# First layer's bias as a 127th row of the units' weights, and one activation per stage

## The chip, the core and the metric

One core of a Trainium2 chip runs the kernel. The metric is the time of one execution on the device in microseconds (us), the median of the runs. All work is inside one launch. The engines are TensorE (PE; its weight loads are the separate row PEld), VectorE (DVE), ScalarE (ACT), GpSimd (POOL), which here issues the gathers, and SyncE (SP), which issues all other transfers. Each engine runs its own list of instructions in order and waits on semaphores that others raise.

## What is computed

The tower of a recommendation model over a batch of 2048. 26 rows of 128 floats are looked up in 26 tables by id; together with the dense features that makes 27 vectors a sample. All pairs of them are multiplied (the interactions), and a three-layer network follows.

```python
e = jnp.stack([tbl_0[ids[:, 0]], ..., tbl_25[ids[:, 25]]], axis=1)
combined = jnp.concatenate([dense_features[:, None, :], e], axis=1)       # 2048 x 27 x 128
interactions = jnp.einsum('bnd,bmd->bnm', combined, combined)
z = jnp.concatenate([dense_features, interactions[:, _TRIU_I, _TRIU_J]], axis=1)
h = jnp.concatenate([z, r_dense_features], axis=1)
h = jnp.maximum(h @ W_top1 + b_top1, 0.0)      # 607 -> 512
h = jnp.maximum(h @ W_top2 + b_top2, 0.0)      # 512 -> 256
y = h @ W_top3                                 # 256 -> 1
```

## The kernel before

The batch is cut into 8 groups of 256 samples, each of two tiles of 128. Of the 26 tables 17 are gathered by GpSimd, one indirect DMA for each table and tile (272 in all, L372), into `rows`, which has a place for each of a group's two tiles. TensorE turns the gathered rows over (`transposes`, L626, five banks a tile), and a place may be filled again once the transposes that read it two tiles earlier are done (the wait in `gather`, L369). The other nine tables, of 1000 rows, are looked up by matmul: VectorE builds a one-hot matrix from the ids (L523), and TensorE multiplies it with the table, split into a high and a low part (`look_up`, L659). ScalarE and VectorE copy the results from PSUM into `embed_t`. TensorE then forms the interactions (`gram`, L689), and ScalarE (L439) and VectorE (L512) copy them out as "units", 14 x 27 = 378 numbers a sample. They go to DRAM and back (`bounce`, L302 and L306), so that they lie as 3 chunks of 126 rows: `packed_raw` in `scratch`.

The network of a group runs during the next group, in seven stages M0 to M6. M0 to M3 are the first layer's four blocks of 128 outputs, M4 and M5 the second layer's two, M6 the last. All float32 products are made of three float32r products (high x high, low x high, high x low; L695 to L697), so each operand is split into a high part (a cast on ScalarE, or an activation with that type) and a low part (VectorE subtracts the high part from the whole, `lower`, L534). A stage M0 to M3 ends with two activations on ScalarE: L401 writes relu(x + b1) in full to `hidden1_raw`, which lies in `scratch`, and L402 the same as `hidden1_hi`; VectorE then makes `hidden1_lo` out of the two. Each stage writes one of two banks of `mlp_ps`, by turns; the bank with the odd stages is also used by the odd ones of the nine look-ups (H1, H3, H5, H7), so a look-up there waits until the stage before it has been copied (L656).

What an engine does in which order is set by one list for all engines, two lines a group, one for each tile:

```python
STEPS = [
    "G0 S0 Q0 H0 M0 Q1 Q2 H1 G1 W0 Q3 H2 W1 M1 Q4 M2 W2 H3 W3".split(),
    "G0 M3 Q0 H4 W4 M4 D0 E0 Q1 Q2 H5 W5 G1 Q3 H6 M5 Q4 H7 H8 M6".split(),
]
```

G is a round of interactions, Q a bank of transposes, H a look-up and the making of a later one-hot, M a stage, S and D the splits of units and dense features, E the dense columns' place in `embed_t`, W the split of a piece of the network's weights, in group 0 only, when there is no stage yet. The last group has a list of its own and two more banks for its stages.

The weights come in once. After the last hot table has been split, SP issues the three loads of `w1_units` (L333), one for each chunk, 126 rows of 512 floats each; two land in `scratch`, one in a buffer of `units`. ScalarE's split of the first one (W0, `weights_upper`, L476) waits for all three: `act.wait_ge(pieces_loaded, 16 * CHUNKS)`. When VectorE has split all three, SP loads `w2` to `scratch`, and when that is split, `w_dense` and `w_again` (L336 to L340).

Of the kernel before, what the change touches and what calls it, by code (L numbers as in the profile page):

```python
# [71 lines left out]
UNIT_P = UNITS * N // CHUNKS  # L72
H1, H2 = 512, 256
# [33 lines left out]
def dlrm_tower(nc, dense_t, ids, hot_ids, row_numbers, tables, w1_dense, w1_again, w1_units, b1, w2, b2, w3, identity, late_rows, bounce, y):  # L107
    ctx = ExitStack()
    with ctx:
# [14 lines left out]
        w1u_hi = sb("w1u_hi", [UNIT_P, CHUNKS, H1], F32R)  # L124
        w1u_lo = sb("w1u_lo", [UNIT_P, CHUNKS, H1], F32R)
# [3 lines left out]
        b1_sb = sb("b1_sb", [P, H1_CHUNKS], F32)  # L129
# [12 lines left out]
        packed_hi = sb("packed_hi", [UNIT_P, BLOCK, CHUNKS, GROUP_BLOCKS], F32R)  # L142
        packed_lo = sb("packed_lo", [UNIT_P, BLOCK, CHUNKS, GROUP_BLOCKS], F32R)
# [14 lines left out]
        hidden1_raw = scratch[:, 0:2, :]  # L158
# [53 lines left out]
        units_lo = sem("units_lo")  # L212
        hidden1_split = sem("hidden1_split")
# [5 lines left out]
        pieces = [(landing[c][0:UNIT_P], w1u_hi[:, c, :], w1u_lo[:, c, :]) for c in range(CHUNKS)]  # L219
# [58 lines left out]
        def _(sp):  # L278
# [45 lines left out]
            sp.dma_start(b1_sb[:, :], b1).then_inc(weights_loaded, 16)  # L324
# [61 lines left out]
        def _(act):  # L386
# [5 lines left out]
            def mlp_copy(g, buf, m):  # L392
# [37 lines left out]
            def units_upper(g, landing=packed_raw):  # L430

                act.wait_ge(units_packed, 16 * (g + 1))
                nc.scalar.copy(packed_hi[:, :, :, :], landing).then_inc(units_hi, 1)
# [40 lines left out]
            def weights_upper(n):  # L474
                if n < CHUNKS:
                    act.wait_ge(pieces_loaded, 16 * CHUNKS)  # L476
                elif n == CHUNKS:
                    act.wait_ge(weights_loaded, 16 * 4)
# [21 lines left out]
            for c in range(CHUNKS):  # L500
                nc.scalar.copy(packed_hi[:, :, c, :], last_packed_raw[:, :, c, :]).then_inc(last_units_hi, 1)
# [4 lines left out]
        def _(dve):  # L506
# [38 lines left out]
            def units_lower(g, landing=packed_raw):  # L545

                dve.wait_ge(units_hi, g + 1)
                lower(landing, packed_hi[:, :, :, :], packed_lo[:, :, :, :]).then_inc(units_lo, 1)

            def hidden1_lower(g, m):  # L550
# [3 lines left out]
                lower(hidden1_raw[:, m % 2, :], hidden1_hi[:, m, :], hidden1_lo[:, m, :]).then_inc(hidden1_split, 1)  # L554

            def group(g, buf, steps, mlp_before=True):
                for t2 in range(TILES):
                    for step, n in [(x[0], int(x[1:])) for x in steps[t2]]:
# [20 lines left out]
                        elif step == "W" and not mlp_before:  # L579

                            dve.wait_ge(weights_loaded, 16 * 6)
# [16 lines left out]

            dve.wait_ge(late_loaded, 16)
# [5 lines left out]
            for c in range(CHUNKS):  # L605
                dve.wait_ge(last_units_hi, c + 1)
                lower(last_packed_raw[:, :, c, :], packed_hi[:, :, c, :], packed_lo[:, :, c, :]).then_inc(last_units_lo, 1)
# [4 lines left out]
        def _(pe):  # L612

            odd_bank = {"tables": 0, "stages": 0}
# [24 lines left out]
            def look_up(g, n):  # L639
# [59 lines left out]
            def mlp(g, buf, m):  # L699
# [36 lines left out]
            def last_mlp():  # L736
# [20 lines left out]
                for part in (range(H1_CHUNKS - 1), range(H1_CHUNKS - 1, H1_CHUNKS)):  # L757
                    for m in range(H1_CHUNKS, H1_CHUNKS + H2_CHUNKS):
                        if part[0] == 0:

                            pe.wait_ge(mlp_copied, MLP_USES * g + m - H1_CHUNKS + 2)
# [40 lines left out]
            pe.wait_ge(weights_loaded, 16 * 6)  # L802
# [63 lines left out]
```

## Time and profile before

| | |
|---|---|
| runs | 392.56, 392.69 and 388.4 us, median 392.56 |
| the profiled execution | span 391.2 us |
| TensorE, its weight loads | 334.4 us busy (85%), 299.1 (76%) |
| VectorE | 260.1 us (66%) |
| ScalarE | 184.1 us (47%) |
| GpSimd | 272.6 us (70%) |
| moved by DMA | 33.28 MB, mean 85 GB/s |

The profile shows one execution. The share of an engine is its busy time over the whole span; how full it is in a part of the program has to be read from a table by stretches. GpSimd's idle time lies in pieces of 0.3 us between gathers. In the chain that ended last, followed back from the end, GpSimd has 40% of the span, TensorE 28%, VectorE 6%, and 16% is "issue", time in which the engine on the chain waited for nothing that the profile shows.

### The profile page before, as it was taken

The page shows a single profiled execution, that of the slowest core. Times are in us where ns is not written, and L with a number is a line of the kernel's source. Part 1 is how long each engine was busy: PE and PEld are TensorE (multiplying, and loading weights), DVE is VectorE, ACT ScalarE, POOL GpSimd, SP SyncE. Part 2 cuts the span into 40 slices and gives each one's busy share as a digit, 9 for nine tenths or more (in the row PEclk, how much of TensorE's full clock was granted, in tenths as well). Part 3 has the DMA queues.
Part 4 walks back from the last instruction along what each step waited for, and adds up shares of the span by engine and source line. Part 5 has one row for each costly group of instructions (what it writes and reads, how often), then busy time and mean ns, then how long its engine had stood idle before and what let it go on. Part 6 is the DMA issues. An engine that isn't in the chain of part 4 may idle for free.

```text
span 391.2 us, 13472 instructions
## 1 busy us (share of the span) xinstructions
PE 334.4 (85%) x6164; PEld 299.1 (76%) x6164; DVE 260.1 (66%) x203; ACT 184.1 (47%) x281; POOL 272.6 (70%) x277
## 2 busy tenths in 40 slices
PE   1866895949999999999998998999989998984847
PEld 1755885839999899889987987878878887873746
DVE  5799697765868876768677765867577665542211
ACT  3454542515464545454554546454535356444314
POOL 6778777777777777777777777777777777773000
PEclk9999998887999999999999999999999999998879
DMA  7971424341225221332133122422133121411020
GB/s 196 263 187 49 129 57 131 97 138 51 57 55 149 57 56 50 116 90 57 49 110 102 51 56 70 139 53 56 50 119 93 50 55 50 141 52 34 3 88 0
DMA packets 19047, 33.28 MB, mean 85 GB/s; under 512 B 5989, under 2 KB 11857, under 8 KB 18992
## 3 DMA queue, kind: packets, MB, share of 16 engines
q0 software_dynamic: 8768, 17.88, 17.5%
q1 hardware_dynamic: 10224, 14.55, 12.6%
q8 instruction: 49, 0.80, 0.9%
q14 instruction: 6, 0.05, 0.0%
HBM read 28.77 MB, written 3.68 MB: 83 GB/s over the span
## 4 chain that ended last, share of the span: by engine, by line
POOL 40%; PE 28%; issue 16%; DMA 6%; DVE 6%; ACT 2%; POOLq 0%; SPq 0%; DVEq 0%
POOL rows L372 40%; PE hot_ps L659 6%; PE mlp_ps L659 5%; PE gram_ps L689 4%; DVE one_hot L523 3%; PE transpose_ps L626 3%; PE mlp_ps L695 3%; DMA rows<-table,ids_sb 3%; PE mlp_ps L696 2%; PE mlp_ps L697 2%; PE hot_ids_ps L635 1%; DVE units L512 1%; DMA scratch<-w 1%; DMA scratch<-w_again 1%; DMA rows<-bounce 1%
## 5 line engine op out<-in xcount | busy, mean ns | idle before, releaser
L372 POOL DMA_INDIRECT rows<-table,ids_sb x272 | 271.7, 999 | 83.4 <-issue 82.3
L523 DVE TENSOR_TENSOR one_hot<-hot_ids_ps,row_numbers_sb 125x2048 fp32r<-125x2048 f32 x72 | 165.0, 2296 | 68.7 <-PE hot_ids_ps L635 62.4
L659 PE MATMUL hot_ps<-one_hot,table_hi 125*128 125x256 f32 x320 | 84.1, 299 | 6.5 <-DVE table_lo L534 4.2
L659 PE MATMUL hot_ps<-one_hot,table_lo 125*128 125x256 f32 x320 | 80.9, 289 | 0.0
L659 PE MATMUL mlp_ps<-one_hot,table_hi 125*128 125x256 f32 x256 | 66.1, 295 | 4.2 <-issue 3.7
L659 PEld LDWEIGHTS hot_ps<-one_hot,table_hi 125*128 125x128 f32 x320 | 63.2, 197 | 8.3 <-issue 8.3
L659 PE MATMUL mlp_ps<-one_hot,table_lo 125*128 125x256 f32 x256 | 63.9, 286 | 0.0
L659 PEld LDWEIGHTS hot_ps<-one_hot,table_lo 125*128 125x128 f32 x320 | 63.4, 198 | 0.0
L626 PE MATMUL transpose_ps<-identity_sb,rows 128*128 128x128 f32 x272 | 46.1, 291 | 18.7 <-DMA rows<-table,ids_sb 13.7
L689 PE MATMUL gram_ps<-embed_t 128*27 128x27 f32 x4096 | 53.5, 195 | 8.8 <-issue 2.3
L390 ACT COPY embed_t<-transpose_ps 128x512 f32<-128x512 f32 (+1 forms) x48 | 54.7, 1139 | 13.2 <-PE transpose_ps L626 12.6
L689 PEld LDWEIGHTS gram_ps<-embed_t 128*27 128x27 f32 x4096 | 44.8, 106 | 19.8 <-issue 13.2
L659 PEld LDWEIGHTS mlp_ps<-one_hot,table_hi 125*128 125x128 f32 x256 | 49.7, 194 | 5.8 <-issue 5.8
L626 PEld LDWEIGHTS transpose_ps<-identity_sb,rows 128*128 128x128 f32 x272 | 30.6, 144 | 28.3 <-DMA rows<-table,ids_sb 22.7
L445 ACT COPY embed_t<-hot_ps 128x256 f32<-128x256 f32 x40 | 27.2, 681 | 51.0 <-PE hot_ps L659 51.0
L512 DVE COPY_PREDICATED units<-late_sb,gram_ps 128x208 f32<-128x208 int32 x32 | 35.3, 1104 | 23.6 <-ACT units L439 23.3
L659 PEld LDWEIGHTS mlp_ps<-one_hot,table_lo 125*128 125x128 f32 x256 | 49.9, 195 | 0.0
L439 ACT COPY units<-gram_ps 128x224 f32<-128x224 f32 x32 | 18.0, 564 | 46.8 <-PE gram_ps L689 46.8
L445 ACT COPY embed_t<-mlp_ps 128x256 f32<-128x256 f32 x32 | 21.9, 683 | 27.6 <-PE mlp_ps L659 27.6
L695 PE MATMUL mlp_ps<-packed_hi,w1u_hi 126*128 126x256 f32 x90 | 26.9, 299 | 7.7 <-DVE packed_lo L534 7.7
L530 DVE COPY embed_t<-transpose_ps 128x384 f32<-128x384 f32 x32 | 32.8, 1025 | 0.0
L696 PE MATMUL mlp_ps<-packed_lo,w1u_hi 126*128 126x256 f32 x90 | 26.1, 291 | 0.0
(70 smaller groups left out, 386.0 us busy)
## 6 DMA issues: line engine op xcount, KB each, us to landing
rows<-table,ids_sb POOLq DMA_INDIRECT x272
embed_t<-table SPq DMA_DIRECT2D x8, 448.0 KB
bounce<-units SPq DMA_DIRECT2D x8, 448.0 KB, 2.7
scratch<-bounce SPq DMA_DIRECT2D x7, 378.0 KB
dense_sb<-dense_t SPq DMA_DIRECT2D x8, 128.0 KB
scratch<-w SPq DMA_DIRECT2D x1, 512.0 KB, 4.0
scratch<-w_units SPq DMA_DIRECT2D x2, 252.0 KB
scratch<-table SPq DMA_DIRECT2D x1, 448.0 KB
```

The source lines that it names most:

```text
L372: nc.gpsimd.indirect_dma_start(rows[:, t2, f - 1, :], None, tables[table], bass.IndirectOffsetOnAxis(ids_sb[:, tile, table:table + 1], 0)) ...
L390: nc.scalar.copy(embed_target(g, t2, u), embed_source(t2, u)).then_inc(even_copied, 1)
L439: nc.scalar.copy(unit_slot(buf, r, 0, UNITS), gram_slot(r, HALF, N)).then_inc(late_copied, 1)
L445: nc.scalar.copy(out, hot_bank(k).rearrange("p (t b) -> p t b", t=TILES)).then_inc(hot_copied, 1)
L512: nc.vector.copy_predicated(unit_slot(buf, r, 1, UNITS), rows_taken, gram_slot(r, 0, HALF)).then_inc(early_copied, 1)
L523: nc.vector.tensor_tensor(one_hot[:, k % RING], ids.to_broadcast([HOT_P, HOT_STEPS, GROUP]), row_numbers_sb[:, :, None].to_broadcast([HOT_ ...
L530: nc.vector.tensor_copy(embed_target(g, t2, u), embed_source(t2, u)).then_inc(odd_copied, 1)
L626: last = nc.tensor.transpose(transpose_ps[:, (t2 * TILE_BANKS + u) % 2, i, :], rows[:, t2, f - 1, :], identity_sb[:, :])
L659: last = nc.tensor.matmul(hot_bank(n), table[:, n, step, :], one_hot[:, k % RING, step, :], start=(step == 0 and table is table_hi), stop= ...
L689: last = nc.tensor.matmul(gram_ps[32 * s:32 * s + N, r % 2, q * N:(q + 1) * N], embed_t[:, slot, b, :], embed_t[:, slot, b, :], start=True ...
L695: nc.tensor.matmul(out, w[0], x[0], start=start, stop=False)
L696: nc.tensor.matmul(out, w[0], x[1], start=False, stop=False)
```

## The change

- The bias of the first layer becomes a 127th row of the units' weights. `w1_units` gets three more rows, one for each chunk: the first holds the bias, the others zeros. The three loads and the splits take 127 rows instead of 126.
- `packed_hi` and `packed_lo` get a 127th row as well, set once by VectorE ahead of group 0: ones in the high part, zeros in the low part. The memsets begin at row 96; the copies of the units write rows 0 to 125 over it later. The matmuls of the units contract over 127 rows instead of 126.
- ScalarE runs one activation in M0 to M3 instead of two (no bias, no `hidden1_raw`), and no longer waits for VectorE there.
- VectorE makes `hidden1_lo` as max(x, 0) minus the high part, with x read from the stage's bank in PSUM.
- So TensorE waits for VectorE's low part where it waited for ScalarE's activation: ahead of stages M2 to M5, and ahead of a look-up in the odd bank.
- The load of the bias, `b1_sb`, is dropped; counts of `weights_loaded` go down by one.

```diff
+BIAS_P = UNIT_P + 1
+ONES_AT = 96
...
-        w1u_hi = sb("w1u_hi", [UNIT_P, CHUNKS, H1], F32R)
+        w1u_hi = sb("w1u_hi", [BIAS_P, CHUNKS, H1], F32R)
...
-        packed_hi = sb("packed_hi", [UNIT_P, BLOCK, CHUNKS, GROUP_BLOCKS], F32R)
+        packed_hi = sb("packed_hi", [BIAS_P, BLOCK, CHUNKS, GROUP_BLOCKS], F32R)
...
-        pieces = [(landing[c][0:UNIT_P], w1u_hi[:, c, :], w1u_lo[:, c, :]) for c in range(CHUNKS)]
+        pieces = [(landing[c][0:BIAS_P], w1u_hi[:, c, :], w1u_lo[:, c, :]) for c in range(CHUNKS)]
...
-            sp.dma_start(b1_sb[:, :], b1).then_inc(weights_loaded, 16)
...
-                    if m >= 2:
-
-                        act.wait_ge(hidden1_split, H1_CHUNKS * g + m - 1)
-                    nc.scalar.activation(hidden1_raw[:, m % 2, :], src, ACT.Relu, bias=b1_sb[:, m:m + 1])
-                    nc.scalar.activation(hidden1_hi[:, m, :], src, ACT.Relu, bias=b1_sb[:, m:m + 1]).then_inc(mlp_copied, 1)
+                    nc.scalar.activation(hidden1_hi[:, m, :], src, ACT.Relu).then_inc(mlp_copied, 1)
...
-                lower(hidden1_raw[:, m % 2, :], hidden1_hi[:, m, :], hidden1_lo[:, m, :]).then_inc(hidden1_split, 1)
+                nc.vector.scalar_tensor_tensor(hidden1_lo[:, m, :], mlp_bank(g, m), 0.0, hidden1_hi[:, m, :].bitcast(F32),
+                                               ALU.max, ALU.subtract).then_inc(hidden1_split, 1)
...
+            nc.vector.memset(packed_hi[ONES_AT:BIAS_P, :, :, :].bitcast(F32), 1.0).then_inc(ones_set, 1)
+            nc.vector.memset(packed_lo[ONES_AT:BIAS_P, :, :, :].bitcast(F32), 0.0).then_inc(ones_set, 1)
...
                     pe.wait_ge(mlp_copied, odd_bank["stages"])
+                    pe.wait_ge(hidden1_split, odd_bank["splits"])
...
+                    odd_bank["splits"] = H1_CHUNKS * g + min(m + 1, H1_CHUNKS)
+                if 2 <= m < H1_CHUNKS + 2:
+
+                    pe.wait_ge(hidden1_split, H1_CHUNKS * g + m - 1)
...
-    w1_units = np.zeros((UNITS * N, H1), w1.dtype)
-    w1_units[where >= 0] = w1[where[where >= 0]]
+    w1_units = np.zeros((UNITS * N + CHUNKS, H1), w1.dtype)
+    w1_units[:UNITS * N][where >= 0] = w1[where[where >= 0]]
+    w1_units[UNITS * N] = a["b_top1"]
```

SP's list around the loads of the weights, before (`w_units` is the DRAM tensor of the units' weights, `w` is w2):

```order
L287 DMA dense_sb<-dense_t 128x256
L333 DMA scratch<-w_units 126x512 [waits lo_split]
L333 DMA scratch<-w_units 126x512
L333 DMA units<-w_units 126x512
L336 DMA scratch<-w 128x4x256 [waits weights_lo]
L339 DMA scratch<-w_dense 128x512 [waits weights_lo]
```

and with the change:

```order
L288 DMA dense_sb<-dense_t 128x256
L333 DMA scratch<-w_units 127x512 [waits lo_split]
L333 DMA scratch<-w_units 127x512
L333 DMA units<-w_units 127x512
L336 DMA scratch<-w 128x4x256 [waits weights_lo]
L339 DMA scratch<-w_dense 128x512 [waits weights_lo]
```

The order and the waits stay; the three loads have a row more each.

TensorE's list at the end of stage M1, then the bank Q4, then M2 and the first matmuls of look-up H3, in group 1, before:

```order
L626 MATMUL transpose_ps<-identity_sb,rows 128x128 [waits even_copied,gathered1_4]
L626 MATMUL transpose_ps<-identity_sb,rows 128x128 x3
L695 MATMUL mlp_ps<-dense_hi,w1d_hi 128x256 [waits mlp_copied]
...
L697 MATMUL mlp_ps<-packed_hi,w1u_lo 128x256
L659 MATMUL mlp_ps<-one_hot,table_hi 128x256 [waits mlp_copied,hot_copied,one_hot_ready]
```

and with the change:

```order
L628 MATMUL transpose_ps<-identity_sb,rows 128x128 [waits even_copied,gathered1_4]
L628 MATMUL transpose_ps<-identity_sb,rows 128x128 x3
L698 MATMUL mlp_ps<-dense_hi,w1d_hi 128x256 [waits hidden1_split,mlp_copied]
...
L700 MATMUL mlp_ps<-packed_hi,w1u_lo 128x256
L662 MATMUL mlp_ps<-one_hot,table_hi 128x256 [waits mlp_copied,hidden1_split,hot_copied,one_hot_ready]
```

No matmul moves; M2 and H3 wait for VectorE's low part (`hidden1_split`) as well.

VectorE's list at the same place, before:

```order
L530 COPY embed_t<-transpose_ps 128x3x128 [waits transposed]
L523 TENSOR_TENSOR one_hot<-hot_ids_ps,row_numbers_sb 125x2048 [waits hot_ids_ready,hot_ready]
L534 TENSOR_TENSOR hidden_lo<-scratch,hidden_hi 128x256 [waits mlp_copied] x2
L523 TENSOR_TENSOR one_hot<-hot_ids_ps,row_numbers_sb 125x2048 [waits hot_ready]
L512 COPY_PREDICATED units<-late_sb,gram_ps 128x16x13 [waits late_copied]
```

and with the change:

```order
L528 COPY embed_t<-transpose_ps 128x3x128 [waits transposed]
L521 TENSOR_TENSOR one_hot<-hot_ids_ps,row_numbers_sb 125x2048 [waits hot_ids_ready,hot_ready]
L552 SCALAR_TENSOR_TENSOR hidden_lo<-mlp_ps,hidden_hi 128x256 [waits mlp_copied] x2
L521 TENSOR_TENSOR one_hot<-hot_ids_ps,row_numbers_sb 125x2048 [waits hot_ready]
L510 COPY_PREDICATED units<-late_sb,gram_ps 128x16x13 [waits late_copied]
```

The low parts of M1 and M2 stand where they stood, behind a one-hot, and read PSUM instead of `scratch`.

## Rows read from the trace of the kernel before

**Rows 1.** Windows: stretch, its us, busy us of each engine, clock, DMA
```profile
88.00:132.00 44.00, 43.60 (x784) 39.49 (x783) 31.06 (x24) 22.49 (x35) 33.33 (x36) 0.95 0.28 76
132.00:352.00 220.00, 206.08 (x4010) 185.24 (x4009) 152.41 (x119) 111.47 (x172) 168.18 (x171) 1.00 0.27 75
```
**Rows 2.** Costliest groups: line, engine, op, count | busy us, mean ns | idle before
```profile
L372 POOL DMA_INDIRECT rows<-table,ids_sb x272 | 271.7, 999 | 83.4 <-issue 82.3
```
**Rows 3.** Waits between 88 and 352 us: total us, times, longest
```profile
PEld transpose_ps L626 <- DMA rows<-table,ids_sb: 12.2, 15, 1.6
PE transpose_ps L626 <- DMA rows<-table,ids_sb: 8.5, 13, 1.3
```
**Rows 4.** Timeline of TensorE: start, us, what, [idle before <-releaser]
```profile
358.71 1.12 PE L626 MATMUL transpose_ps<-identity_sb,rows 128*128 128x128 f32 x4 [3.91 <-DMA rows<-table,ids_sb]
```
**Rows 5.** Timeline: the sixth tile's first gather; transposes two tiles earlier
```profile
116.69 1.12 POOL L372 DMA_INDIRECT rows<-table,ids_sb  x1 [0.30 <-issue]
...
87.68 0.90 PE L626 MATMUL transpose_ps<-identity_sb,rows 128*128 128x128 f32 x3
```
**Rows 6.** Timeline of SP: the first two of the three loads
```profile
39.09 0.76 SPq L333 DMA_DIRECT2D scratch<-w_units  x2
```
**Rows 7.** DMA, 38 to 46 us: busy tenths, SP's queue (packets, MB, share)
```profile
DMA  0056000000837689998998997998440290010090
...
q1 hardware_dynamic: 420, 0.77, 32.1%
```
**Rows 8.** DMA, 66 to 70 us, SP's queue: w_dense and w_again
```profile
q1 hardware_dynamic: 288, 0.52, 37.0%
```
**Rows 9.** DMA, 390 to 392 us, SP's queue: the last result's store
```profile
q1 hardware_dynamic: 2, 0.00, 0.2%
```
**Rows 10.** DMA queues over the span: the gathers' queue
```profile
q0 software_dynamic: 8768, 17.88, 17.5%
```
**Rows 11.** Timeline of ScalarE: the first cast of the units' weights
```profile
51.60 0.64 ACT L482 CAST w1u_hi<-scratch 126x512 fp32r<-126x512 f32 x1
```
**Rows 12.** Timeline of VectorE: from the first to the third weights' part
```profile
54.59 0.92 DVE L534 TENSOR_TENSOR w1u_lo<-scratch,w1u_hi 126x512 fp32r<-126x512 f32 x1
55.42 0.94 DVE L530 COPY embed_t<-transpose_ps 128x384 f32<-128x384 f32 x1
56.20 2.28 DVE L523 TENSOR_TENSOR one_hot<-hot_ids_ps,row_numbers_sb 125x2048 fp32r<-125x2048 f32 x1
58.41 0.66 DVE L534 TENSOR_TENSOR w1u_lo<-scratch,w1u_hi 126x512 fp32r<-126x512 f32 x1
59.00 0.67 DVE L534 TENSOR_TENSOR w1u_lo<-units,w1u_hi 126x512 fp32r<-126x512 f32 x1
```
**Rows 13.** Groups by form: the activation that the change removes
```profile
L401 ACT ACTIVATE scratch<-mlp_ps,b_sb 128x256 f32<-128x256 f32 x30 | 14.3, 475 | 24.7 <-PE mlp_ps L697 24.7
```
**Rows 14.** Timeline around H3 in the second group of the network
```profile
145.00 0.28 PE L659 MATMUL mlp_ps<-one_hot,table_hi 125*128 125x256 f32 x1
...
143.50 2.29 DVE L523 TENSOR_TENSOR one_hot<-hot_ids_ps,row_numbers_sb 125x2048 fp32r<-125x2048 f32 x1
145.71 0.84 DVE L534 TENSOR_TENSOR hidden_lo<-scratch,hidden_hi 128x256 fp32r<-128x256 f32 x2
```
**Rows 15.** The same place four groups later
```profile
316.47 0.28 PE L659 MATMUL mlp_ps<-one_hot,table_hi 125*128 125x256 f32 x1
...
316.47 0.40 DVE L534 TENSOR_TENSOR hidden_lo<-scratch,hidden_hi 128x256 fp32r<-128x256 f32 x1
```
**Rows 16.** The last group's last low part, and TensorE's first use of it
```profile
385.33 0.42 DVE L534 TENSOR_TENSOR hidden_lo<-scratch,hidden_hi 128x256 fp32r<-128x256 f32 x1 [0.65 <-ACT hidden_hi L402]
...
386.42 0.28 PE L695 MATMUL mlp_ps<-hidden_hi,w_hi 128*128 128x256 f32 x1
```
**Rows 17.** A memset on VectorE, and its idle time ahead of group 0's work
```profile
L584 DVE MEMSET gram_ps<- 128x1024 f32 x1 | 0.9, 912 | 1.0 <-PEq L858 1.0
...
44.83 2.29 DVE L523 TENSOR_TENSOR one_hot<-hot_ids_ps,row_numbers_sb 125x2048 fp32r<-125x2048 f32 x1 [3.56 <-PE hot_ids_ps L635]
```

More of the change, by code:

```diff
@@ L104, with dlrm_tower @@
 FIRST_STEPS = "H0 Q0 H1 Q1 H2 H3 Q2 H4 H5 Q3 H6 H7 Q4 E0 H8".split()
-def dlrm_tower(nc, dense_t, ids, hot_ids, row_numbers, tables, w1_dense, w1_again, w1_units, b1, w2, b2, w3, identity, late_rows, bounce, y):
+def dlrm_tower(nc, dense_t, ids, hot_ids, row_numbers, tables, w1_dense, w1_again, w1_units, w2, b2, w3, identity, late_rows, bounce, y):
     ctx = ExitStack()
@@ L123, in dlrm_tower @@
         w1d_lo = sb("w1d_lo", [P, H1], F32R)
-        w1u_hi = sb("w1u_hi", [UNIT_P, CHUNKS, H1], F32R)
-        w1u_lo = sb("w1u_lo", [UNIT_P, CHUNKS, H1], F32R)
+        w1u_hi = sb("w1u_hi", [BIAS_P, CHUNKS, H1], F32R)
+        w1u_lo = sb("w1u_lo", [BIAS_P, CHUNKS, H1], F32R)
         w2_hi = sb("w2_hi", [P, H1_CHUNKS, H2], F32R)
@@ L212, in dlrm_tower @@
         units_lo = sem("units_lo")
+        ones_set = sem("ones_set")
         hidden1_split = sem("hidden1_split")
@@ L432, in units_upper @@
                 act.wait_ge(units_packed, 16 * (g + 1))
-                nc.scalar.copy(packed_hi[:, :, :, :], landing).then_inc(units_hi, 1)
+                if g == 0:
+                    act.wait_ge(ones_set, 2)
+                nc.scalar.copy(packed_hi[0:UNIT_P, :, :, :], landing).then_inc(units_hi, 1)
             def late_columns(g, buf, r):
@@ L477, in weights_upper @@
                 elif n == CHUNKS:
-                    act.wait_ge(weights_loaded, 16 * 4)
+                    act.wait_ge(weights_loaded, 16 * 3)
                 else:
@@ L500, in _ @@
             for c in range(CHUNKS):
-                nc.scalar.copy(packed_hi[:, :, c, :], last_packed_raw[:, :, c, :]).then_inc(last_units_hi, 1)
+                nc.scalar.copy(packed_hi[0:UNIT_P, :, c, :], last_packed_raw[:, :, c, :]).then_inc(last_units_hi, 1)
             for m in range(MLP_USES):
@@ L547, in units_lower @@
                 dve.wait_ge(units_hi, g + 1)
-                lower(landing, packed_hi[:, :, :, :], packed_lo[:, :, :, :]).then_inc(units_lo, 1)
+                lower(landing, packed_hi[0:UNIT_P, :, :, :], packed_lo[0:UNIT_P, :, :, :]).then_inc(units_lo, 1)
             def hidden1_lower(g, m):
                 dve.wait_ge(mlp_copied, MLP_USES * g + m + 2)
-                lower(hidden1_raw[:, m % 2, :], hidden1_hi[:, m, :], hidden1_lo[:, m, :]).then_inc(hidden1_split, 1)
+                nc.vector.scalar_tensor_tensor(hidden1_lo[:, m, :], mlp_bank(g, m), 0.0, hidden1_hi[:, m, :].bitcast(F32),
+                                               ALU.max, ALU.subtract).then_inc(hidden1_split, 1)
             def group(g, buf, steps, mlp_before=True):
@@ L579, in group @@
                         elif step == "W" and not mlp_before:
-                            dve.wait_ge(weights_loaded, 16 * 6)
+                            dve.wait_ge(weights_loaded, 16 * 5)
                             nc.vector.tensor_tensor(w1d_sb, w1d_sb, w1a_sb, ALU.add).then_inc(w1_summed, 1)
@@ L606, in _ @@
                 dve.wait_ge(last_units_hi, c + 1)
[L607 removed]
+                lower(last_packed_raw[:, :, c, :], packed_hi[0:UNIT_P, :, c, :], packed_lo[0:UNIT_P, :, c, :]).then_inc(last_units_lo, 1)
             for m in range(H1_CHUNKS):
@@ L612, in _ @@
         def _(pe):
-            odd_bank = {"tables": 0, "stages": 0}
+            odd_bank = {"tables": 0, "stages": 0, "splits": 0}
             ids_bank = {"next": None}
@@ L759, in last_mlp @@
                         if part[0] == 0:
-                            pe.wait_ge(mlp_copied, MLP_USES * g + m - H1_CHUNKS + 2)
+                            pe.wait_ge(hidden1_split, H1_CHUNKS * g + m - H1_CHUNKS + 1)
                         h = slice((m - H1_CHUNKS) * P, (m - H1_CHUNKS + 1) * P)
@@ L800, in _ @@
             group(0, 0, STEPS, first=True)
-            pe.wait_ge(weights_loaded, 16 * 6)
+            pe.wait_ge(weights_loaded, 16 * 5)
             pe.wait_ge(weights_lo, len(pieces))
```

6 lines of the change are left out of this document (2 added, 4 removed).

## The prediction

> **What bounds the kernel now.** I read the busy time by stretches first. From 88 to 132 us TensorE is busy 43.6 of 44 us; from 132 to 352 us it is busy 206.1 of 220 [rows 1]. Then the costliest groups: GpSimd issues 272 gathers, 271.7 us busy and 83.4 us idle before them, of which 82.3 us carry the label "issue", that is, they wait for nothing [rows 2]. Together 355.1 us, 1.305 us a gather and 44.4 us for the 34 gathers of a group. So GpSimd never stops until about 357 us and sets the pace of the second half: the waits show TensorE waiting 8.5 us for gathered rows before its transposes between 88 and 352 us, and its weight loads 12.2 us for the same reason [rows 3]; before the very last transposes it waits another 3.91 us [rows 4]. After that comes a tail of some 32 us of one group's own work. Until 88 us neither is full: tables and weights arrive, and ScalarE and VectorE split them.
>
> Does a gather ever wait for TensorE? The first gather of the sixth tile (tiles counted from one) starts at 116.69 us, and it may start once the transposes that read its place two tiles earlier are done, which was at 88.58 (87.68 + 0.90) [rows 5]. So GpSimd has about 28 us in hand there. TensorE can be set back by up to 28 us before a gather is.
>
> **The change, part by part.**
>
> *The bias row in the load of the units' weights.* SP issues three loads of 126 rows at 39.09 us and just after [rows 6]; now each has 127 rows. The DMA rows of before show how a transfer of SP's queue is shared out, since each engine that takes part ends with a small packet of its own. Between 38 and 46 us SP's queue (q1) moved 420 packets [rows 7]: 3 x 126 = 378 rows of weights and 42 more, 14 for each load. Between 66 and 70 us it moved 288 [rows 8]: the 256 rows of w_dense and w_again and 32 more, 16 for each. The result's store, one row, is 2 packets [rows 9], one of them data. So 128 rows go to 16 engines, 126 to 14, 1 to 1: the largest number up to 16 that divides the rows. Shares of eight rows would have put 126 rows on 16 engines, and they are not there. 127 is prime, so I expect all three loads, 381 rows of 2 KB, on one engine.
>
> The Trainium skill says this outright (DMA: Bandwidth & Descriptors, "Why a DMA increments its semaphore by 16 and not by 1"): the number of engines is the largest up to 16 that divides the slowest dimension of both sides, and it names 127 partitions as a case with one engine. By that rule the trace's counts come out as they do; no row here shows 127.
>
> How long is that? Price of a 2 KB packet: from [rows 8], 37.0% of 16 engines over 4 us is 23.7 engine-us for 256, 0.0925 us each; from [rows 7], 32.1% over 8 us is 41.1 engine-us for 378, 0.109 us each. I take the first, since with one engine at work fewer packets crowd the memory. 381 x 0.0925 = 35.2 us. The gathers take 17.5% of every engine's time [rows 10] and will take it on this one too: 35.2 / 0.825 = 42.7 us. Bounds: 35.2 (gathers cost nothing) and 381 x 0.109 / 0.825 = 50.3. Before, the packets ran from about 40.0 us (the 11th of the 40 slices of 0.2 us) to 43.7 [rows 7]. So the last weights land at 82.7 us (75.2 to 90.3) instead of 43.7.
>
> The same page ("Where 436 GB/s comes from") gives 16 ports at 435 GB/s in all, 27 GB/s for one; as an estimate, 780 KB would take 28.7 us by it and the whole kernel would come out near 398 us. The traces have shown only 22 GB/s for 2 KB packets, so I don't go by it.
>
> Who waits? ScalarE's first cast of these weights waits for all three loads; before it began at 51.60 us [rows 11], 8 us after they were there, so the wait was free. Now ScalarE stands still from 51.60 to 82.7. Behind that cast, in its queue, are the copies of the looked-up and the transposed rows. VectorE stops at its part of the same weights, and TensorE finishes the two look-ups and the transposes that it has and then waits for ScalarE's copies at the next interactions. A little is made up: from the first cast to the end of VectorE's third part of the weights it was 8.1 us (51.60 to 59.67) [rows 11, 12], with work among it that will have been done while waiting; what is left is the cast, 0.64, and VectorE's 0.92, 0.94, 2.28, 0.66 and 0.67, 6.1 us. Behind it stand the load of w2, then w_dense and w_again, one after the other as before. TensorE is set back by 82.7 - 51.6 - 2.0 = 29.1 us.
>
> *GpSimd* may run two tiles ahead, so it goes on issuing; 29.1 against 28 of slack is at most a stop of 1 to 3 us, and TensorE, later still, doesn't see it.
>
> *What is made up afterwards.* TensorE no longer waits for rows: 8.5 to 12.2 us [rows 3], I take 10, and 3.9 at the end [rows 4]. The rest of its work is back to back and can't be shortened.
>
> *One activation instead of two.* 32 activations go, 475 ns each [rows 13], 15 us of ScalarE, which is not what anything waits for in the steady part.
>
> *The low part straight from PSUM.* VectorE's subtraction took 0.42 us (0.84 for two) [rows 14]. A PSUM operand shows in the one-hots, 2.29 us for 2048 columns, 0.29 for 256 [rows 14]; with a start of its own a subtraction from PSUM lies between 0.42 and 0.7 us. I take 0.45. But the bank is now free only after it, so TensorE waits for VectorE where it waited for ScalarE. The place is the look-up of the fourth table (H3), which writes the bank of stage M1. It started at 145.00; VectorE, behind a one-hot of 2.29 us, ended M1's low part at 146.13 (145.71 + 0.42) [rows 14]. That is 1.1 us, in the group where TensorE was full; in a late group the two were 316.47 and 316.87, 0.4 us [rows 15]. With TensorE the bound all along I take 0.9 for each of the six groups from the third: 5.4 us (0 to 7). For the other stages the low part was ready long before the bank was wanted. In the last group each stage has a bank of its own, and its last low part is ready at 385.75, 0.7 us before the 386.42 at which it is read [rows 16]; the saved activation wins nothing there.
>
> *Two memsets* of 31 x 768 on VectorE: 128 x 1024 took 0.91 us, and VectorE idles 3.56 us right where they stand [rows 17]. Nothing. With no idle there they would cost up to 1.8 us. The dropped load of the bias is one of SP's issues in a stretch where SP is ahead: nothing. The bias row adds no matmul.
>
> **Sum**, against the profiled execution (span 391.2 us): 391.2 + 29.1 - 10 - 3.9 + 5.4 = 411.8. That execution lies 1.4 us under the median of the runs, 392.56; I say 412.
>
> **The rivals.**
> - *The load is shared out after all* (127 rows over 14 to 16 engines, unevenly). For it: no row shows a count other than 1, 14 and 16. Against it: the 14 engines for 126 rows. Then the weights land at 43.7 us with 8 us in hand, and what is left is H3's wait, 1.1 us a group at most, while GpSimd has 28 us in hand and TensorE makes it up before 352 us. 391 us, 389 to 394. It decides from a landing at about 51.6 us: 11.5 us for the load, three engines or more. Chance 10%.
> - *The one engine is slower still*: the gathers' packets of 4 KB take turns with the 2 KB ones, and other traffic lands there too, so that the load takes 60 us. For it: in [rows 7] a packet cost 18% more than in [rows 8]. Against: gathers come only every 1.3 us. Landing at 100 us, TensorE back by 46 us, GpSimd stopped for 18 us, still less than TensorE: 391.2 + 46.4 - 13.9 + 5.4 = 429. Chance 5%.
> - *ScalarE's relief matters*: 15 us less work lets its copies come earlier, and the kernel gets faster with the load shared out. Where TensorE waits in the steady part it waits for rows and not for ScalarE's copies [rows 3], so at best 1 to 2 us at the tail: 389. Chance 2%.
>
> My forecast has 83%.
>
> **How the numbers follow.** Forecast, with its own bounds: landing at 75.2 gives 404, at 90.3 gives 419.5; without H3's wait it is 5.4 less, with 14 us made up 4 less. 401 to 425 holds nearly all of its 83% and leaves out the other three. Slower by over 2% (about what a measurement of this kernel can tell from no change) in the forecast and the second rival, 88%; within 2% in the first rival, 10%; faster 2%, which is generous.
>
> **What would show it.** Right: SP's queue moves 384 packets for the three loads, 3 of them small, from 40 to about 83 us; ScalarE's first cast of the weights stands behind 25 to 38 us of waiting for that DMA; VectorE and TensorE stand still beside it; TensorE never waits for rows after 130 us; H3 waits for VectorE's new instruction by about 1 us a group. Wrong: 420 or more packets for those loads and a cast at 51.6 us (then the first rival), or TensorE waiting for rows in the second half (then GpSimd was stopped longer than thought).

## The result and the profile after

The changed kernel took 408.88 us (median of 4 runs, 407.52 to 410.26) against 391.65 for the kernel before in the same runs: a ratio of 1.044, 95% interval 1.040 to 1.049. It is slower, by 17 us. Single executions come out some per cent slower than the rest, and the ratios in this document leave them out, so a ratio need not be the quotient of two medians. The profiled execution has a span of 405.7 us, 14.5 more than the 391.2 of before.

Of the page of the kernel after, the gathers' queue (packets, MB, share of 16 engines), the chain that ended last by engine and by line, and the gathers' group:

```profile
q0 software_dynamic: 8768, 17.88, 16.8%
...
PE 60%; DVE 19%; DMA 12%; ACT 4%; issue 3%; SPq 2%; DVEq 0%
PE hot_ps L662 12%; PE mlp_ps L662 12%; PE gram_ps L692 12%; DVE one_hot L521 10%; DMA units<-w_units 8%; PE mlp_ps L698 5%; PE transpose_ps L628 5%; PE mlp_ps L699 4%; PE mlp_ps L700 4%; PE hot_ids_ps L637 3%; DVE units L510 2%; DVE table_lo L532 2%; PE mlp_ps L739 2%; DVE embed_t L528 1%; DVE packed_lo L532 1%
...
L372 POOL DMA_INDIRECT rows<-table,ids_sb x272 | 269.1, 989 | 83.5 <-issue 79.9
```

GpSimd had 40% of the chain before and is gone from it. Its gathers are as long as they were [rows 2]. In their place stands TensorE, and a load of the units' weights with 8% of the span, 32 us, which wasn't on the list at all.

The kernel after, its DMA queues between 38 and 78 us:

```profile
q0 software_dynamic: 995, 2.03, 19.2%
q1 hardware_dynamic: 384, 0.78, 5.1%
```

And SP's timeline in the same stretch (start, us, what), its issues of the three loads:

```profile
39.43 4.18 SPq L333 DMA_DIRECT2D scratch<-w_units  x2
43.66 11.73 SPq L333 DMA_DIRECT2D units<-w_units  x1
```

Before, it was 420 packets, 32.1% of 16 engines in 8 us [rows 7]. Now 384 packets, 381 rows and 3 small ones, take 5.1% of 16 engines in 40 us: 0.82 of one engine. One small packet a load, so one engine a load; and all three on the same one, since three engines side by side would have been done after a third of the 35.7 us that the 2 KB packets took (40.2 to 75.9 us).

What stood behind it, from the timelines of ScalarE and VectorE, and of TensorE at its next interactions (start, us, what, idle before and its releaser):

```profile
52.01 0.54 ACT L437 COPY units<-gram_ps 128x224 f32<-128x224 f32 x1 [1.37 <-PE gram_ps L692]
76.34 0.62 ACT L480 CAST w1u_hi<-scratch 127x512 fp32r<-127x512 f32 x1 [23.79 <-DMA units<-w_units]
76.86 0.66 ACT L443 COPY embed_t<-hot_ps 128x256 f32<-128x256 f32 x1
...
76.99 0.69 DVE L532 TENSOR_TENSOR w1u_lo<-scratch,w1u_hi 127x512 fp32r<-127x512 f32 x1 [20.66 <-ACT w1u_hi L480]
...
79.06 1.99 PE L692 MATMUL gram_ps<-embed_t 128*27 128x27 f32 x128 [20.91 <-ACT embed_t L390]
```

The first cast stood at 51.60 us before and waited for nothing [rows 11]. ScalarE now stands 23.79 us for the DMA, VectorE 20.66 for ScalarE, TensorE 20.91 for a copy that waits in ScalarE's queue behind the cast.

The steady part of the kernel after, as one window from 132 to 352 us: busy us in the order TensorE, its loads, VectorE, ScalarE, GpSimd.

```profile
132.00:352.00 220.00, 210.09 (x4039) 188.97 (x4038) 157.80 (x120) 103.60 (x153) 167.27 (x174) 1.00 0.27 76
```

And the longest waits of TensorE proper between 88 and 352 us, in the kernel after (sum in us, count, longest):

```profile
PE mlp_ps L662 <- DVE hidden_lo L552: 6.0, 6, 1.1
...
PE transpose_ps L628 <- ACT embed_t L390: 3.3, 1, 3.3
```

The waits for gathered rows [rows 3] are gone, none is left between 88 and 352 us. TensorE is 210.1 us busy instead of 206.1 [rows 1] and has a new wait, six times about 1 us (1.1 the longest), for VectorE's low part ahead of the fourth look-up. One of the six, in the second group of the network:

```profile
162.93 2.28 DVE L521 TENSOR_TENSOR one_hot<-hot_ids_ps,row_numbers_sb 125x2048 fp32r<-125x2048 f32 x1
165.14 0.73 DVE L552 SCALAR_TENSOR_TENSOR hidden_lo<-mlp_ps,hidden_hi 128x256 fp32r<-128x256 f32 x2
...
165.69 0.36 PE L662 MATMUL mlp_ps<-one_hot,table_hi 125*128 125x256 f32 x1 [1.12 <-DVE hidden_lo L552]
```

The look-up starts when the first of the two low parts is done; before it did not look at them [rows 14]. TensorE's granted clock is 1.00 in this stretch before and after, so it isn't a slower clock that holds TensorE up there.

### The profile page after: what moved, and what is told of

Read it like the earlier page. It is cut to its first block, busy times and chain, and to the rows that moved or that the text cites. A ratio compares the mean times of both kernels' runs of the same rounds, so it can differ in the third digit from the quotient of the medians.

```text
span 405.7 us, 13456 instructions
## 1 busy us (share of the span) xinstructions
PE 333.5 (82%) x6164; PEld 298.3 (74%) x6164; DVE 260.1 (64%) x205; ACT 169.2 (42%) x249; POOL 270.0 (67%) x277
## 3 DMA queue, kind: packets, MB, share of 16 engines
q0 software_dynamic: 8768, 17.88, 16.8%
q1 hardware_dynamic: 10044, 14.55, 12.0%
## 4 chain that ended last, share of the span: by engine, by line
PE 60%; DVE 19%; DMA 12%; ACT 4%; issue 3%; SPq 2%; DVEq 0%
PE hot_ps L662 12%; PE mlp_ps L662 12%; PE gram_ps L692 12%; DVE one_hot L521 10%; DMA units<-w_units 8%; PE mlp_ps L698 5%; PE transpose_ps L628 5%; PE mlp_ps L699 4%; PE mlp_ps L700 4%; PE hot_ids_ps L637 3%; DVE units L510 2%; DVE table_lo L532 2%; PE mlp_ps L739 2%; DVE embed_t L528 1%; DVE packed_lo L532 1%
## 5 line engine op out<-in xcount | busy, mean ns | idle before, releaser
L692 PE MATMUL gram_ps<-embed_t 128*27 128x27 f32 x4096 | 54.6, 196 | 30.9 <-ACT embed_t L390 22.7
L692 PEld LDWEIGHTS gram_ps<-embed_t 128*27 128x27 f32 x4096 | 45.7, 107 | 42.3 <-ACT embed_t L390 23.1
L628 PE MATMUL transpose_ps<-identity_sb,rows 128*128 128x128 f32 x272 | 44.4, 288 | 6.4 <-ACT embed_t L390 3.3
L698 PE MATMUL mlp_ps<-packed_hi,w1u_hi 127*128 127x256 f32 x90 | 27.4, 304 | 7.0 <-DVE packed_lo L532 7.0
L699 PE MATMUL mlp_ps<-packed_lo,w1u_hi 127*128 127x256 f32 x90 | 26.4, 293 | 0.0
```

The source lines that it names most:

```text
L628: last = nc.tensor.transpose(transpose_ps[:, (t2 * TILE_BANKS + u) % 2, i, :], rows[:, t2, f - 1, :], identity_sb[:, :])
L692: last = nc.tensor.matmul(gram_ps[32 * s:32 * s + N, r % 2, q * N:(q + 1) * N], embed_t[:, slot, b, :], embed_t[:, slot, b, :], start=True ...
L698: nc.tensor.matmul(out, w[0], x[0], start=start, stop=False)
L699: nc.tensor.matmul(out, w[0], x[1], start=False, stop=False)
```

## The experiments

Four questions: is the 127-row load the cause (e1, f1, e4, f4), how much lateness of the weights can be made up (e2, f2, e3, f3), what the wait of the look-ups costs (f4, g1, h1, g2), and whether the number of engines depends on the queue (g3). The e kernels ran on one chip and the g kernels on another, on which the kernel before itself takes 549.64 and 547.99 us (the median of all its runs there); what these two slow chips can and can't say stands with them. The f kernels and h1 ran where the kernel before takes 391.61 and 390.23 us.

**e1_split and f1_split: each load cut into 126 rows and 1.**

```diff
             for c in range(CHUNKS):
-                sp.dma_start(pieces[c][0], w1_units.rearrange("(p c) h -> c p h", c=CHUNKS)[c]).then_inc(pieces_loaded, 16)
+                for r in ([slice(0, 126), slice(126, 127)], [slice(0, 126), slice(126, 127)], [slice(0, 126), slice(126, 127)])[c]:
+                    sp.dma_start(pieces[c][0][r], w1_units.rearrange("(p c) h -> c p h", c=CHUNKS)[c][r]).then_inc(pieces_loaded, 16)
...
-                    act.wait_ge(pieces_loaded, 16 * CHUNKS)
+                    act.wait_ge(pieces_loaded, 16 * 6)
```

> The changed kernel, with each of the three loads of the units' weights cut into 126 rows and 1 row. Theory (the 127-row load runs on one engine, and that is the whole loss): SP's queue moves the 381 rows with 14 + 1 small packets a load, 426 packets in all, the rows are there by about 45 us, ScalarE's first cast stands at about 52 us without a wait for a DMA, and the time is that of the kernel before, 391 us (389 to 394); the wait of the fourth look-up for VectorE, about 1 us a group, stays and is made up. Rival (the waits for VectorE's low part cost the time, the load is only a companion): 6 us or more above before, 397 to 400.

e1_split took 547.81 us, ratio 1.011 (1.004 to 1.020). Its time decides little between the two forecasts, as the waits of e1_split show: TensorE waited 126.5 us with nothing but "issue" as the cause, in 160 pieces before its small interaction matmuls.

```profile
POOL rows L373 <- PE transpose_ps L629: 134.3, 38, 6.7
PE gram_ps L693 <- issue: 126.5, 160, 2.6
```

On this chip GpSimd waits for TensorE, 134.3 us, so the bound is another than in the kernel that the forecasts are about. The DMA counts are of use all the same: 426 packets, as expected (381 rows, 14 + 1 small ones a load). The same kernel on the chip of the f kernels:

> The changed kernel, with each of the three loads of the units' weights cut into 126 rows and 1 row: the kernel of e1_split, on a chip where the kernel before has its own time. Theory (the one-engine load is the whole loss): 391 us (389 to 394), the first cast at about 52 us without a wait for a DMA, TensorE waiting for rows in the second half as before. Rival (the waits for VectorE's low part cost the time): 397 to 400.

390.65 us (10 runs) against 391.61, ratio 0.999 (0.995 to 1.003). The profile of f1_split, SP's queue from 38 to 46 us:

```profile
q1 hardware_dynamic: 426, 0.78, 31.9%
```

ScalarE's first cast in f1_split:

```profile
52.67 0.63 ACT L481 CAST w1u_hi<-scratch 127x512 fp32r<-127x512 f32 x1
```

Everything else of the change is in this kernel, and the loss is gone: without these three loads' shape there is none. But TensorE isn't where it was, as the waits of f1_split's whole execution show:

```profile
PEld transpose_ps L629 <- DMA rows<-table,ids_sb: 2.3, 2, 1.6
PE transpose_ps L629 <- DMA rows<-table,ids_sb: 1.9, 2, 1.4
...
PE mlp_ps L663 <- DVE hidden_lo L553: 6.0, 6, 1.1
```

Over the whole execution it waits 1.9 us for rows, where between 88 and 352 us alone it was 8.5 before [rows 3]; I had expected these waits to stay as they were. The look-ups' wait costs no time, but it has used up most of what TensorE had in hand.

**e2_two_engines and f2_two_engines: 122 rows and 5. e3_two_whole and f3_two_whole: two loads of 127, the third 126 and 1.**

Against f1_split, first in e2 and f2, then in e3 and f3 (where ScalarE waits for `16 * 4`):

```diff
-                for r in ([slice(0, 126), slice(126, 127)], [slice(0, 126), slice(126, 127)], [slice(0, 126), slice(126, 127)])[c]:
+                for r in ([slice(0, 122), slice(122, 127)], [slice(0, 122), slice(122, 127)], [slice(0, 122), slice(122, 127)])[c]:
```

```diff
-                for r in ([slice(0, 126), slice(126, 127)], [slice(0, 126), slice(126, 127)], [slice(0, 126), slice(126, 127)])[c]:
+                for r in ([slice(0, 127)], [slice(0, 127)], [slice(0, 126), slice(126, 127)])[c]:
```

> The changed kernel, with each load cut into 122 rows and 5 rows. If the number of engines is the largest up to 16 that divides the rows, 122 rows go to 2 engines: 183 rows of 2 KB on each at 35.65 / 381 = 0.094 us, 17 us, so that the weights are there at 57 us and the first cast stands 5 us later than its place at 52 us. TensorE makes 2 us of that up at once and the rest later: 391 to 393 us. Small packets: 2 + 5 a load, 402 packets in all. Rival (shares of whole blocks of rows, 16 engines for 122): 429 packets, no wait at the cast.

> The changed kernel, with two of the loads whole (127 rows) and the third cut into 126 and 1. Theory: 254 rows and a share of 9 more on one engine, 263 x 0.094 = 24.6 us, weights there at 65 us, the first cast 13 us late, TensorE 10 to 11 us late after it. Of that 14 us can be made up where TensorE waited for rows, less 5 us for the fourth look-ups: 391 + 10.7 - 13.9 + 5.4 = 393 us, 391 to 396. Rival (every us of lateness of the weights comes out at the end, nothing is made up): 402 us.

Both ran on the first slow chip, 546.32 and 547.22 us, ratios 1.003 (0.994 to 1.012) and 1.004 (0.998 to 1.009), and say nothing on time. e2's queue moved 402 packets between 38 and 80 us, as expected: 381 rows, 2 + 5 small ones a load. The rule "largest number up to 16 that divides the rows" holds for 122 as for 126 and 127, and shares of whole blocks are ruled out.

> The changed kernel, with each load cut into 122 rows (two engines, as the packet counts of e2_two_engines showed) and 5 rows: the weights are there at about 57 us, the first cast 5 us late, and all of it is made up: 391 to 393 us. Rival (nothing is made up): 395 to 397.

> The changed kernel, with two of the loads whole (127 rows, one engine) and the third cut into 126 and 1: weights there at about 65 us, first cast 13 us late, TensorE 10 to 11 us late after it, of which nearly all is made up where TensorE waited for rows: 393 us, 391 to 396. Rival (nothing is made up): 402.

f2: 392.45 us, ratio 1.004 (1.000 to 1.008). f3: 396.61 us, ratio 1.014 (1.008 to 1.020), 0.6 us above the range that I had given and 3.6 us over my figure. ScalarE's first cast in f2 and in f3:

```profile
58.90 0.62 ACT L481 CAST w1u_hi<-scratch 127x512 fp32r<-127x512 f32 x1 [5.62 <-DMA units<-w_units]
```

```profile
65.89 0.62 ACT L481 CAST w1u_hi<-scratch 127x512 fp32r<-127x512 f32 x1 [13.82 <-DMA units<-w_units]
```

The lateness is near what was computed (5.6 and 13.8 us of waiting, computed 5 and 13). Of the 5.6 nearly all was made up (spans 390.7 and, for f1, 390.0), of the 13.8 less than expected: it cost 5.1 (span 395.1).

**e4_before_127 and f4_before_127: the kernel before with the 127-row loads alone.**

```diff
-                sp.dma_start(pieces[c][0], w1_units.rearrange("(p c) h -> c p h", c=CHUNKS)[c]).then_inc(pieces_loaded, 16)
+                sp.dma_start(landing[c][0:BIAS_P], w1_units.rearrange("(p c) h -> c p h", c=CHUNKS)[c]).then_inc(pieces_loaded, 16)
...
-    w1_units = np.zeros((UNITS * N, H1), w1.dtype)
-    w1_units[where >= 0] = w1[where[where >= 0]]
+    w1_units = np.zeros((UNITS * N + CHUNKS, H1), w1.dtype)
+    w1_units[:UNITS * N][where >= 0] = w1[where[where >= 0]]
```

> The kernel before, with one thing of the change alone: w1_units has three more rows, and the three loads take 127 rows instead of 126 (the 127th isn't used; the bias stays where it was). Theory: the first cast waits until 76 us as in the changed kernel, TensorE is late by the same 19 to 23 us, but the fourth look-ups don't wait for VectorE, about 1 us in each of six groups: 6 us less than the changed kernel, 401 to 404 us. Rival (the load is not the cause): 391 us. Rival (the load is all of it, the look-ups' wait costs nothing even when TensorE is the bound): 408 us.

> The kernel before with the three loads of 127 rows alone (the 127th row unused): first cast at about 76 us as in the changed kernel, TensorE as late, but no wait of the fourth look-ups for VectorE: 6 us less than the changed kernel, 401 to 404 us. Rival (the load is not the cause): 391. Rival (the look-ups' wait costs nothing): 408.

e4 took 551.48 us on the first slow chip, ratio 1.003 (0.995 to 1.011), undecided. f4: 400.63 us (4 runs, 399.78 to 403.17), ratio 1.024 (1.018 to 1.029), 0.4 us below the range of the forecast and far from both rivals. So one row more in three loads, which nobody reads, costs 9 us; the changed kernel loses 17. ScalarE's first cast in f4:

```profile
79.02 0.62 ACT L483 CAST w1u_hi<-scratch 126x512 fp32r<-126x512 f32 x1 [26.31 <-DMA units<-w_units]
```

And f4's steady part, as a window:

```profile
132.00:352.00 220.00, 215.76 (x4145) 195.61 (x4143) 163.53 (x125) 114.72 (x178) 167.88 (x172) 1.00 0.28 76
```

The weights are even later than in the changed kernel (26.3 against 23.8 us of waiting, the cast at 79.02 us where I had expected 76), and yet the profiled execution, the slowest of the four, ends 4.5 us sooner. TensorE is 215.8 us of 220 busy, in the changed kernel 210.1. The difference of 5.7 us is near the 5.1 us that it waits for low parts in this stretch; that these waits are the reason is what the next two kernels test.

**g1_m1_first and h1_m1_first: the late loads stay, VectorE makes M1's low part ahead of the one-hot.**

```diff
             def group(g, buf, steps, mlp_before=True):
+                if mlp_before and steps is STEPS:
+                    steps = ["G0 S0 Q0 H0 M0 Q1 Q2 H1 G1 Q3 M1 H2 Q4 M2 H3".split(), STEPS[1]]
                 for t2 in range(TILES):
```

This is in VectorE's block alone and works in groups 1 to 6: the one-hot of H2 moves behind the low part of M1, and the steps W, which do nothing after group 0, are left out. f4 differs from the changed kernel in several things, this kernel in one.

> The changed kernel with its late loads of 127 rows, but from group 1 on VectorE makes the low part of stage M1 ahead of the one-hot that stands before it, so that the fourth look-up finds its bank free. Theory (the look-ups' wait and the late weights draw on the same slack of TensorE, and 8 us of the changed kernel's loss are this wait's): no wait of TensorE's look-ups for VectorE's low part, and 401 us (399 to 403), that of f4_before_127. Rival (the 8 us between the changed kernel and f4_before_127 come from something else, the memsets or the subtraction from PSUM): 408 us.

g1 took 550.77 us on the second slow chip, ratio 1.007 (1.003 to 1.011), which doesn't decide between the forecasts.

> The kernel of g1_m1_first once more, wanted on a chip where TensorE is not held up by its own instructions: the changed kernel with its late loads of 127 rows, and VectorE making M1's low part ahead of the one-hot. Theory (the look-ups' wait and the late weights draw on the same slack of TensorE): no wait of TensorE's look-ups for VectorE's low part, 401 us (399 to 403) where the kernel before takes 391.6. Rival (the 8 us between the changed kernel and f4_before_127 come from the memsets or from the subtraction out of PSUM): 408 us.

402.11 us (4 runs) against 390.23, ratio 1.031 (1.023 to 1.038), where the changed kernel has 1.044 (1.040 to 1.049). In the profile of h1 (span 399.9) the cast waits 23.09 us, 0.7 less than in the changed kernel, and among TensorE's waits none for a hidden layer's low part is left. Two that are there:

```profile
PE mlp_ps L664 <- ACT scratch L402: 1.7, 3, 0.6
PE mlp_ps L700 <- DVE packed_lo L532: 1.2, 5, 0.5
```

h1's window from 132 to 352 us:

```profile
132.00:352.00 220.00, 213.96 (x4074) 192.99 (x4074) 162.20 (x122) 105.93 (x156) 167.04 (x174) 1.00 0.29 80
```

The six waits are gone and 5.8 us of span with them (the weights came 0.7 us sooner, which is part of it); the subtraction from PSUM and the memsets are still in it. Where these 5.8 us arise shows in the starts of one round of interactions, near the end of the steady part, in the kernel before, in the changed one and in h1:

```profile
341.63 1.38 PE L689 MATMUL gram_ps<-embed_t 128*27 128x27 f32 x112
```

```profile
358.94 1.24 PE L692 MATMUL gram_ps<-embed_t 128*27 128x27 f32 x126
```

```profile
352.38 1.25 PE L694 MATMUL gram_ps<-embed_t 128*27 128x27 f32 x126
```

TensorE is 17.3 us late here in the changed kernel and 10.8 in h1. At the round that before starts at 128.77 us it was 19.3 and 18.1 (148.07 and 146.88). So the changed kernel made up 2.0 us in between and h1 7.4, with the same loads: 5.4 us of the difference belong to the look-ups' wait. By the times, the two kernels lie 17.2 and 11.9 us over before and f4 9.0; the last 2.9 us, in which the subtraction and the memsets may have a part, are inside the intervals of h1 and f4, and nothing here separates them.

**g2_split_m1_first: both repairs, and the memsets at the head of VectorE's list.**

The edits are those of f1 and g1; the two memsets stand right behind that of `gram_ps`.

> Both repairs and the memsets moved to the head of VectorE's list: loads cut into 126 rows and 1, the low part of M1 ahead of the one-hot. Theory: GpSimd's gathers are the bound again and TensorE gets its waits for rows back (about 10 us instead of 1.9 in f1_split), which wins nothing: 390 to 391 us, as f1_split. Rival (f1_split was held up a little by TensorE): 387 to 389.

It ran on the second slow chip only: 549.87 us, ratio 1.004 (1.000 to 1.007). Whether it would gain anything over f1_split where GpSimd is the bound stays open.

**g3_load_by_gpsimd: the three loads issued by GpSimd.**

```diff
             for tile in range(TILE_COUNT):
+                if tile == 2:
+                    pool.wait_ge(lo_split, HOT)
+                    for c in range(CHUNKS):
+                        nc.gpsimd.dma_start(pieces[c][0], w1_units.rearrange("(p c) h -> c p h", c=CHUNKS)[c]).then_inc(pieces_loaded, 16)
                 gather(tile)
```

> The changed kernel, with the three loads of 127 rows issued by GpSimd, ahead of the third tile's gathers at about 51 us, instead of by SP. If the number of engines follows the same rule on GpSimd's queue: each load on one engine again, perhaps each on another, so 127 x 0.094 = 12 us if side by side, weights at 66 us, 396 to 398 us; 35 us one after the other, weights at 88 us, about 418 us. If GpSimd's queue shares 127 rows over 16 engines: weights at 57 us, 392 to 394 us, GpSimd about 3 us later with its gathers for the three issues.

Also on the second slow chip: 545.63 us, ratio 0.990 (0.982 to 0.997). That is 1% under the kernel before, by few runs and on a chip where another bound holds; it doesn't test the forecasts, and where the kernel before takes 391 us it wasn't run. The queues over the whole execution of g3:

```profile
q0 software_dynamic: 9008, 18.66, 12.8%
q1 hardware_dynamic: 9660, 13.77, 8.3%
```

SP's queue has the 384 packets of the changed kernel less (10044 there). GpSimd's has 240 more than the 8768 of before [rows 10]. 780 KB in packets of up to 4 KB, two rows each, are 64 a load, 192; the other 48 are 16 for each load. So on GpSimd's queue the same 127 rows went to 16 engines. The 16 engines together are 90% busy for a good microsecond just behind the three issues (63.09 to 64.74 us), as this row of tenths from 60 to 70 us shows; one engine would make less than one tenth, and the gathers alone two:

```profile
DMA  0000000000000000093699999794552093000900
```

**What all of it adds up to.** The first column is ScalarE's wait for the weights, the third the span over that of the kernel with loads in time (391.2 for those without the look-ups' wait, 390.0, f1, for those with it), the last the difference, what was made up. Each row is one profiled execution; runs of one kernel lie 3 to 6 us apart, so single microseconds here mean little.

| | wait for weights | look-ups' wait | span over | made up |
|---|---|---|---|---|
| f2_two_engines | 5.6 | yes | 0.7 | 4.9 |
| f3_two_whole | 13.8 | yes | 5.1 | 8.7 |
| the changed kernel | 23.8 | yes | 15.7 | 8.1 |
| h1_m1_first | 23.1 | no | 8.7 | 14.4 |
| f4_before_127 | 26.3 | no | 10.0 | 16.3 |

The kernel can make up 14 to 16 us of late weights: with the weights in time TensorE waits for GpSimd's rows, and in the late kernels it doesn't. The look-ups' wait alone costs nothing (f1), for it is paid out of the same store. Together they overdraw it: with the wait only 8 to 9 us are left, and beyond that each us of lateness is about a us of time (from f3 to the changed kernel 10.0 us later, 10.6 us longer). Where the kernel before takes 391 us, no version that was run beats it; f1_split equals it.

## Why the prediction was right

Forecast 412 us, 401 to 425; measured 408.88. The sum behind the forecast was of the span, 411.8, and the span is 405.7. Step by step:

- *The bound before* (GpSimd's gathers, TensorE with something in hand) held: f1_split, with all of the change but the load's shape, has the time of before, though TensorE has less in hand there.
- *One engine for 127 rows.* Right, 384 packets. The rule read from 14, 16 and 1 small packets was borne out by 122 and 127 as well. The Trainium skill's sentence on 127 partitions (DMA: Bandwidth & Descriptors, "Why a DMA increments its semaphore by 16 and not by 1") agrees.
- *How long the load takes.* The term that was too big: I had 42.7 us, and the 2 KB packets ran from 40.2 to 75.9 us, 35.7. I had taken 0.0925 us a packet [rows 8] and divided by 0.825 for the gathers' share. Between 38 and 78 us the one engine gave 32.6 us (5.1% of 16 over 40 us) to 384 packets, 0.085 us each; that is 91% of the 35.7 us. So both the price and what I had taken off for the gathers were too high here, and the lower bound, 35.2, is where it came out. The price isn't fixed: in f4 it was 0.091 (5.2% over 42 us). The first cast stood at 76.34 instead of 82.7, 6.4 us of too much.
- *Set back and made up at once.* I had TensorE late by the wait less 2.0 us. The first bank of the third tile's transposes began at 58.89 before and at 81.59 now, 22.7 us later, where the term would have given 22.7 (76.34 - 51.6 - 2.0). Right to a tenth.
- *GpSimd doesn't matter.* Right: nine stops for TensorE, none above 0.3 us, 2.7 us in all.
- *Made up later.* By the fifth tile's first bank (109.91 before, 129.18 now) TensorE was 19.3 us late: 3.4 us had been made up between 60 and 110 us, where I had allowed nothing (TensorE's clock was 0.87 in that piece of work before and 0.92 now). From there to the sixteenth tile (343.37 and 362.36) it stayed 19.0, where I had netted 4.6 us of gain (10 less 5.4). The waits for rows that fell away there were 8.5 us and not 10. Five of the look-ups' six waits took 5.1 us of them, 1.2 went to longer waits of the look-ups for ScalarE (1.7 instead of 0.5), and 2.0 to one stop right ahead of that bank, for which the profile names no cause:

```profile
362.22 0.21 PE L692 MATMUL gram_ps<-embed_t 128*27 128x27 f32 x2 [2.04 <-issue]
```

  f1 and h1 have such a stop at the same place in the work (1.5 and 2.2 us), the kernel before and f4 don't; what it is stays open. The last bank's transposes ended at 359.8 before and at 375.2 now, 15.4 us later: 3.6 of the forecast 3.9 us [rows 4] were made up. The tail, at which I had expected nothing, was 0.9 us shorter (30.5 instead of 31.4).
- *The look-ups' wait.* I had 0.9 us for each of six, 5.4; the wait itself was 6.0 us, and taking it away gave 5.8 us of span, of which 0.7 may be the earlier weights (h1).
- *The memsets.* The place was wrong. They don't stand in VectorE's 3.56 us of idle time but behind the one-hot that ends it, as VectorE's timeline of the kernel after shows:

```profile
45.13 2.29 DVE L521 TENSOR_TENSOR one_hot<-hot_ids_ps,row_numbers_sb 125x2048 fp32r<-125x2048 f32 x1 [3.52 <-PE hot_ids_ps L637]
47.64 0.70 DVE L599 MEMSET packed_hi<- 31x768 f32 x1 [0.22 <-issue]
48.45 0.70 DVE L600 MEMSET packed_lo<- 31x768 f32 x1
49.17 1.10 DVE L510 COPY_PREDICATED units<-late_sb,gram_ps 128x208 f32<-128x208 int32 x1
```

  With their gaps they hold VectorE for 1.8 us (47.42 to 49.17), the price that I had named for the case without cover. Here the wait for the weights hides it. In f1_split the first cast is 1.1 us later than before (52.67 against 51.60), which may come from them, and that is made up.
- *One activation, and the subtraction from PSUM.* Both right in kind: ScalarE has 15 us less work (169.2 instead of 184.1), and f1, which has that too, is no faster than before. The subtraction takes 447 ns, I had 450.

The mechanism was right, and the nearness of the number is in part luck. Against the forecast span the load gave 6.4 us less and the early stretch 3.4 less, the steady part 4.3 more and the end 0.3 more, the tail 0.9 less: 6.1 us less together, of which the steady part's error hides 4.3. And half of these 6.1 don't show in the time, since the median of the runs lies 3.2 us above the profiled span, where I had added 0.2.

## What to carry to other kernels

Before a transfer gets a row more, count the engines that it will run on: 126, 122 and 127 rows went to 14, 2 and 1 engines of SP's queue, and a load that had been 8 us early came 24 us late. Here a row wanted in addition cost nothing once it was loaded by a transfer of its own (f1). And slack is one account: two changes that are each free because an engine has something in hand are not free together, so say for each what it takes from which account, and not only whether it is covered.

## What was not expected of the hardware

- The queue decides too. 127 rows went to one engine from SP and to 16 from GpSimd (g3), with two 2 KB rows to a packet there.
- SP was held in issuing where few engines took the load: two loads took 4.18 us and the third 11.73 us, where the first two took 0.76 us before [rows 6]. In f4 it was 4.28 and 12.62 us, in f2, on two engines, 4.40 and 5.58, in f1 1.29 and 0.62. Nothing else was due on SP then. That a transfer behind them would have been late follows from SP's order, but no run tests it.
- The activation became shorter as well as single. The one of the same form before, and two groups of the kernel after:

```profile
L402 ACT ACTIVATE hidden_hi<-mlp_ps,b_sb 128x256 fp32r<-128x256 f32 x30 | 14.0, 468 | 0.0
```

```profile
L398 ACT ACTIVATE hidden_hi<-mlp_ps 128x256 fp32r<-128x256 f32 x30 | 11.5, 385 | 25.7 <-PE mlp_ps L700 25.7
...
L552 DVE SCALAR_TENSOR_TENSOR hidden_lo<-mlp_ps,hidden_hi 128x256 fp32r<-128x256 f32 x30 | 12.9, 447 | 9.1 <-ACT hidden_hi L398 9.1
```

  385 ns without a bias tile, 468 with one (475 where the result was a plain float32 [rows 13]). The Trainium skill (ScalarE: Activation LUTs, "What ACT_TABLE_LOAD costs") gives about 93 ns for such an operand; the 83 ns here are near it.
- The same kernel took 547.81 us on one chip (e1) and 390.65 on another (f1). In e1 TensorE stood 126.5 us before the small matmuls of the interactions with nothing but "issue" as the cause, in f1 4.7, and the mean granted clock was 0.82 and 0.97. Why the chips differ is not shown. The late load could not be told from none in the time there: e4's ratio was 1.003, f4's 1.024.
